# A mixture of experts ahead of three convolution layers: two images per product, gates multiplied into the patches, expert outputs summed feature-major in one PSUM bank

## The reference

```
xp = patches of the normed x                  # 16 * 256 patches, d = 128 features
probs = softmax(xp @ router_w)                # 8 experts
gate = the two largest of probs, divided by their sum, zero elsewhere
for e in range(8):
    val, g = split(xp @ w1[e])                # 2 x 256 hidden features
    out += gate[:, e] * ((val * sigmoid(g)) @ w2[e])
```

## Time and profile before

| | |
|---|---|
| median of 3 runs | 1914.44 us (1912.62 to 1920.05) |
| span of the profiled execution, the time of this execution | 2385.4 us |
| PE busy, products | 1477.8 us (62%) |
| DVE busy | 902.8 us (38%) |
| ACT busy | 513.5 us (22%) |
| POOL busy | 1200.2 us (50%), of it 1147.6 in 1152 gathers |
| mean granted clock of PE | 0.782 of full |

### The profile page before, as it was taken

The page is one execution under the profiler, slowest core; times in us unless marked ns, Lnnn a source line. Parts: engine busy times, 40 slices in busy tenths (PEclk is TensorE's granted clock), DMA queues, the critical chain, the costliest instruction groups (busy, mean ns, idle before and its releaser), DMA issues.

```text
span 2385.4 us, 17778 instructions
## 1 busy us (share of the span) xinstructions
PE 1477.8 (62%) x5782; PEld 846.0 (35%) x5782; DVE 902.8 (38%) x1416; ACT 513.5 (22%) x823; POOL 1200.2 (50%) x1393
## 2 busy tenths in 40 slices
PE   6973323465257966774578985674339684138988
PEld 5842222353133433542244443542114231013433
DVE  3532322234242332575332333576313227441235
ACT  2220000112022223112322322112302221023343
POOL 7126675556744644565654654465664546740000
PEclk9976555677578988886678998786669886568999
DMA  4021111112121111112131111112131111111000
GB/s 169 1 56 43 41 51 39 39 34 80 52 65 35 41 29 35 38 38 76 49 74 32 41 37 33 34 47 66 51 80 32 37 32 43 53 32 44 1 0 9
DMA packets 66784, 106.71 MB, mean 45 GB/s; under 512 B 20480, under 2 KB 43904, under 8 KB 66304
## 3 DMA queue, kind: packets, MB, share of 16 engines
q0 software_dynamic: 36864, 75.57, 11.8%
q1 hardware_dynamic: 29248, 26.81, 4.0%
q10 hardware_dynamic: 576, 3.15, 0.3%
HBM read 83.16 MB, written 13.89 MB: 41 GB/s over the span
## 4 chain that ended last, share of the span: by engine, by line
PE 35%; another core or an unknown queue 28%; issue 14%; DVE 9%; ACT 5%; POOL 3%; DMA 1%; DVEq 0%; SPq 0%; ACTq 0%; POOLq 0%
PE bank L1326 9%; PE bank L1311 8%; PE bank L1226 4%; POOL gt L635 3%; PE bank L1357 3%; PE bank L1236 2%; DVE gt L1038 2%; DVE rb L1117 2%; PE bank L1331 2%; PE bank L1266 2%; PE bank L1344 1%; PE bank L1288 1%; PE bank L1385 1%; DVE gt L1039 1%
## 5 line engine op out<-in xcount | busy, mean ns | idle before, releaser
L635 POOL DMA_INDIRECT gt<-corner_table,idx x1152 | 1147.6, 996 | 920.0 <-DVE sm L1044 490.9
L1226 PE MATMUL bank<-xp,w_sb 128*128 128x256 f32 x1024 | 310.4, 452 | 119.1 <-issue 50.9
L1326 PE MATMUL bank<-yg,wts 128*128 128x512 f32 x512 | 257.3, 647 | 46.9 <-ACT tg L758 38.1
L1226 PEld LDWEIGHTS bank<-xp,w_sb 128*128 128x128 f32 x1024 | 221.5, 229 | 179.1 <-issue 66.2
L1311 PE MATMUL bank<-u,wk 128*128 128x512 f32 x512 | 240.9, 620 | 9.0 <-DMA u<-sqb 9.0
L941 DVE SCALAR_TENSOR_TENSOR he<-he,bank 128x512 f32<-128x512 f32 x128 | 87.7, 685 | 399.2 <-ACT he L692 194.1
L1236 PE MATMUL bank<-w_sb,he 128*128 128x128 f32 x1024 | 159.5, 301 | 115.5 <-issue 101.8
L1357 PE MATMUL bank<-xp,musq 128*128 128x512 f32 x212 | 131.0, 765 | 145.5 <-issue 82.4
L1236 PEld LDWEIGHTS bank<-w_sb,he 128*128 128x128 f32 x1024 | 154.8, 216 | 129.8 <-issue 120.6
L1288 PE MATMUL bank<-cst,sm 128*128 128x128 f32 x384 | 82.5, 330 | 189.2 <-DVE sm L1044 84.5
L1038 DVE TENSOR_TENSOR gt<-gt,cw 128x1152 f32<-128x1152 f32 x128 | 173.2, 1353 | 52.9 <-DMA gt<-corner_table,idx 35.4
(11 more groups left out here) (185 smaller groups left out, 1258.2 us busy)
## 6 DMA issues: line engine op xcount, KB each, us to landing
gt<-corner_table,idx POOLq DMA_INDIRECT x1152
corner_table<-tb SPq DMA_DIRECT2D x45, 256.0 KB, 5.6
u<-sqb SPq DMA_DIRECT2D x64, 128.0 KB
w_sb<-w ACTq DMA_DIRECT2D x2, 1024.0 KB, 9.2
out<-X SPq DMA_DIRECT2D x8, 256.0 KB
X<-x SPq DMA_DIRECT2D x1, 1536.0 KB, 18.8
wts<-weights SPq DMA_DIRECT2D x1, 1446.0 KB, 15.3
w_sb<-w ACTq DMA_DIRECT2D x2, 512.0 KB, 12.1
```

What stands on the lines that cost most here:

```text
L635: pool.indirect_dma_start(gt[:, g, k].rearrange("p a c -> p (a c)"), None, table, bass.IndirectOffsetOnAxis(ap=idx[:, j, g * KK + k:g * KK ...
L1226: op = mm(psum[b][:, h * TOK:(h + 1) * TOK], w1_sb[:, e, first + h], xp[:, g], start=True, stop=True)
L1326: op = mm(psum[B2.bank(name)][:, :], w_glu[:, k, col + d * P:col + (d + 1) * P], yg[:, c % 2, k], start=k == 0, stop=k == NB2 - 1)
```

## The change

A unit is now (pair of images q, expert e, half h of the hidden features), again 32 of them. Gate, value and output are one product of 512 columns each. The gate weights no longer scale the output: before the experts, PE turns the gates so that (patch block, expert) lies on 64 partitions, DVE spreads them to `shares` (64 x 1024) with one block of columns for each block of patches, and for each pair and expert one more product, "share", with a one-hot column as weights, broadcasts a row of gates to 128 partitions of bank 0; DVE multiplies `xp` by it into `xg`, which feeds the value product. The outputs, features on partitions, of all eight experts and both halves add up in bank 2 over 16 units, so `acc` and its additions are gone. ACT copies the bank twice a slice; 16 products with 32 columns of the identity as weights put the features back on the channels' partitions, and DVE adds in two instructions of 512 elements. The order has one part more, `l0_gates`, ahead of the units, and steps 0 to 2 of sampling hold seven parts. Constants grow by 16 columns.

```diff
@@ -19,7 +19,7 @@
-NU = GI * NE
+NU = 2 * NE * 2
@@ -40,7 +40,7 @@
-A_PLACES = [(0, 2, 6), (2, 17, 9), (17, 22.5, NU + 2 - 15), (22.5, 23.6, 2), (25.2, 27.8, 3 + TQ - 2)]
+A_PLACES = [(0, 2, 7), (2, 17, 9), (17, 22.5, NU + 2 - 15), (22.5, 23.6, 2), (25.2, 27.8, 3 + TQ - 2)]
@@ -144,12 +144,12 @@
 def plan_a():
-    plan = [(("xp", 0), 0), (("xp", 1), 1), ("router", 2)]
+    plan = [(("xp", 0), 0), (("xp", 1), 1), ("router", 2), ("turned", 2), (("share", 0), 0)]
     for u in range(NU):
         plan += [(("gate", u), 0), (("value", u), 1)]
-        if u:
-            plan.append((("out", u - 1), 2))
-    plan += [(("out", NU - 1), 2), (("back", 0), 0), (("back", 1), 1)]
+        if u % 2 and u < NU - 1:
+            plan.append((("share", u // 2 + 1), 0))
+    plan += [(("out", q), 2) for q in range(2)] + [(("back", 0), 0), (("back", 1), 1)]
     head = [("omc", 0), ("omc", 1), ("table", 0), ("table", 1), ("om", 0), ("om", 1)]
@@ -181,7 +181,7 @@
-    parts = [("l0_unit", u) for u in range(NU + 1)] + [("l0_tail",), ("l1_norm",), ("l1_conv",), ("l1_om",)]
+    parts = [("l0_gates",)] + [("l0_unit", u) for u in range(NU + 1)] + [("l0_tail",), ("l1_norm",), ("l1_conv",), ("l1_om",)]
@@ -320,9 +320,9 @@
-        acc = sb("acc", [P, 2, PT * PT, GI, C])
-
-        xn0 = acc[:, :, :, :, :].rearrange("p t a g c -> p (t a g c)")
+        xg = sb("xg", [P, 2, HALF])
+
+        xn0 = xg[:, :, :].rearrange("p i n -> p (i n)")
@@ -346,7 +346,10 @@
-        omt = acc[:, :, :, :, :].rearrange("p t a g c -> p (t a g c)")
+        omt = xg[:, :, :].rearrange("p i n -> p (i n)")
+
+        shares = cwn[0:8 * NE, :, :, :].rearrange("p t k a -> p (t k a)")[:, 0:8 * P]
+        oT = [t[:, :, :].rearrange("p t k -> p (t k)")[:, 0:HALF] for t in (fl, fr)]
@@ -686,10 +689,18 @@
                     return
+                if u == NU // 2 + 1:
+                    l0_result(s, 0)
                 B0.filled(act, s, ("gate", u))
-                if u >= 2:
-                    B0.filled(act, s, ("out", u - 2))
+                if u == NU // 2 + 1:
+                    B0.filled(act, s, ("out", 0))
+                elif u >= 2:
+                    act.wait_ge(S["he_used"], s * (NU - 2) + u - 1 - (u - 2) // (NU // 2))
                 act.activation(he[:, u % 2], psum[0][:, :], ACT.Tanh, scale=0.5).then_inc(free[0], 1)
+
+            def l0_result(s, q):
+                B0.filled(act, s, ("out", q))
+                act.activation(oT[q], psum[2][:, :], ACT.Copy).then_inc(free[2], 1)
@@ -932,44 +943,42 @@
-                ch.then(stt(out=gate[:, :, :], in0=gate[:, :, :], scalar=0.5, in1=over(m1),
-                            op0=ALU.mult, op1=ALU.mult))
-
-            def l0_he(s, u):
+                stt(out=gate[:, :, :], in0=gate[:, :, :], scalar=0.5, in1=over(m1),
+                    op0=ALU.mult, op1=ALU.mult).then_inc(S["gate_ready"], 1)
+
+            def l0_gates(s):
+
+                B0.filled(dve, s, "turned")
+                op = tt(shares.rearrange("p (t n) -> p t n", t=8),
+                        psum[2][0:8 * NE, 0:P].unsqueeze(1).to_broadcast([8 * NE, 8, P]),
+                        con("token")[0:8 * NE].unsqueeze(2).to_broadcast([8 * NE, 8, P]), ALU.mult)
+                op.then_inc(free[2], 1)
+                l0_share(s, 0)
+
+            def l0_share(s, i):
+
+                q = i // NE
+                B0.filled(dve, s, ("share", i))
+                tt(xg[:, i % 2], xp[:, 2 * q:2 * q + 2].rearrange("p g n -> p (g n)"), psum[0][:, :], ALU.mult)\
+                    .then_inc(free[0], 1)
+
+            def l0_unit(s, u):
+                if u == NU:
+                    return
                 B0.filled(dve, s, ("value", u))
...
                     op0=ALU.add, op1=ALU.mult).then_inc(free[1], 1)
-
-            def l0_acc(s, u):
-                g, e = divmod(u, NE)
-                B0.filled(dve, s, ("out", u))
-                if e:
-                    B0.read(dve, s, ("out", u - 1))
-                for t in range(2):
-                    sc = gate[:, g * 2 + t, e:e + 1]
-                    o = psum[2][:, t * D0:(t + 1) * D0].rearrange("p (a c) -> p a c", c=C)
-                    a = acc[:, t, :, g]
-                    if e:
-                        op = stt(out=a, in0=o, scalar=sc, in1=a, op0=ALU.mult, op1=ALU.add)
-                    else:
-                        op = ts(a, o, sc, None, ALU.mult)
-                    if t:
-                        op.then_inc(free[2], 1)
+                if u % 2 and u < NU - 1:
+                    l0_share(s, u // 2 + 1)
             def l0_tail(s):
-                for t in range(2):
-                    B0.filled(dve, s, ("back", t))
-                    for dy in range(PT):
-                        xv = X[:, bass.ds(s, 1), :].rearrange("p o (h a w b) -> p (o h) a b w", a=PT, b=PT,
-                                                              w=W // PT)
-                        xv = xv[:, t * 8:(t + 1) * 8, dy].rearrange("p h b w -> p b h w")
-                        bk = psum[t][:, dy * 2 * P:(dy + 1) * 2 * P].rearrange("p (b h w) -> p b h w", b=PT, h=8)
-                        op = tt(xv, xv, bk, ALU.add)
-                        if dy:
-                            op.then_inc(free[t], 1)
-                        else:
-                            ch.did(op)
+                xv = X[:, bass.ds(s, 1), :].rearrange("p o (h a w b) -> p (o h) a b w", a=PT, b=PT, w=W // PT)
+                for dy in range(PT):
+                    B0.filled(dve, s, ("back", dy))
+                    xd = xv[:, :, dy].rearrange("p h b w -> p b h w")
+                    bk = psum[dy][:, :].rearrange("p (b h w) -> p b h w", b=PT, h=H // PT)
+                    tt(xd, xd, bk, ALU.add).then_inc(free[dy], 1)
                 B0.read(dve, s, ("back", 0))
@@ -1218,35 +1221,57 @@
+            def l0_gates(s):
+
+                pe.wait_ge(S["gate_ready"], s + 1)
+                B0.vacant(pe, s, "turned")
+                hold(pe)
+                pe.transpose(psum[2][0:8 * NE, 0:P], gate[:, :, :].rearrange("p t e -> p (t e)"), ident)\
+                  .then_inc(full[2], 1)
+                B0.read(pe, s, "turned")
+                l0_share(s, 0)
+
+            def l0_share(s, i):
+
+                q, e = divmod(i, NE)
+                B0.vacant(pe, s, ("share", i))
+                mm(psum[0][:, :], con("expert")[0:8 * NE, e:e + 1].to_broadcast([8 * NE, P]),
+                   shares[:, q * HALF:(q + 1) * HALF], start=True, stop=True).then_inc(full[0], 1)
+
             def l0_h(s, u):
-                g, e = divmod(u, NE)
-                for kind, b, first in (("gate", 0, 2), ("value", 1, 0)):
-                    B0.vacant(pe, s, (kind, u))
-                    for h in range(2):
-                        op = mm(psum[b][:, h * TOK:(h + 1) * TOK], w1_sb[:, e, first + h], xp[:, g],
-                                start=True, stop=True)
-                    op.then_inc(full[b], 1)
+
+                i, h = divmod(u, 2)
+                q, e = divmod(i, NE)
+                B0.vacant(pe, s, ("gate", u))
+                mm(psum[0][:, :], w1_sb[:, e, 2 + h], xp[:, 2 * q:2 * q + 2].rearrange("p g n -> p (g n)"),
+                   start=True, stop=True).then_inc(full[0], 1)
+                B0.read(pe, s, ("share", i))
+                B0.vacant(pe, s, ("value", u))
+                mm(psum[1][:, :], w1_sb[:, e, h], xg[:, i % 2], start=True, stop=True).then_inc(full[1], 1)
+                if h and u < NU - 1:
+                    l0_share(s, i + 1)
             def l0_out(s, u):
-                g, e = divmod(u, NE)
+                i, h = divmod(u, 2)
+                q, e = divmod(i, NE)
                 B0.read(pe, s, ("value", u))
-                B0.vacant(pe, s, ("out", u))
-                for t in range(2):
-                    for h in range(2):
-                        op = mm(psum[2][:, t * D0:(t + 1) * D0],
-                                he[:, u % 2, h * TOK + t * P:h * TOK + (t + 1) * P], w2_sb[:, e, h],
-                                start=h == 0, stop=h == 1)
-                op.then_inc(full[2], 1)
+                if u % (NU // 2) == 0:
+                    B0.vacant(pe, s, ("out", q))
+                last = u % (NU // 2) == NU // 2 - 1
+                mm(psum[2][:, :], w2_sb[:, e, h], he[:, u % 2], start=u % (NU // 2) == 0, stop=last)\
+                    .then_inc(full[2] if last else S["he_used"], 1)
             def l0_tail(s):
-                B0.read(pe, s, ("out", NU - 1))
-                for t in range(2):
-                    B0.vacant(pe, s, ("back", t))
-                    for dyx in range(4):
-                        op = pe.transpose(psum[t][:, dyx * P:(dyx + 1) * P],
-                                          acc[:, t, dyx].rearrange("p g c -> p (g c)"),
-                                          ident)
-                    op.then_inc(full[t], 1)
+                for q in range(2):
+                    B0.read(pe, s, ("out", q))
```

(30 more changed lines are left out.)

## The result

The kernel after takes 1957.11 us (median of 4 runs, 1955.34 to 1961.69); the kernel before, beside it, 1913.53 us (1911.65 to 1920.05). The ratio is 1.0229, 95% interval 1.0205 to 1.0252: slower by 43.6 us.

A forecast was written before the change was run, and what follows sets the result against it. PE bounds the uncovered head, the gathers' pace nearly bounds the middle. The median 1914.4 plus 20.5 for the head and 18 for two slices gives 1953 us; range 1908 to 1985, the forecast's own 1938 to 1972.

The forecast's parts named there:

- The 471 us: Profiled execution's excess over the runs' median, read mostly as PE holes while gathers run, which ordinary runs lack.
- Head, 20.5 us: First slice's layers 0 and 1 before the first gather: PE-bound, uncovered, 20.5 us longer; bounds 14 to 26.
- The pair: Two units of the first layer in the head: 6.11 us after the change, 3.06 a unit, +0.44 each.
- Middle, 18 us: Two slices with layers 2 and 3 beside them: PE's extra work costs 9 us each, between 0 and 12.3.
- the ring of four: Four places for gathered tiles in the middle: hides PE or DVE lateness up to three steps, 33.7 us.
- the 67 us: Runs' median above head, gathers at 1.248 us and tail; taken as a sign the ring is partly used up.
- DVE's 7.2 us at nothing: DVE works 7.2 us less a slice: worth nothing in the head, in the middle only where DVE ends last.
- B: Only the head counts, the middle stays at the gathers' pace: 1935 us; chance 0.20.
- C: Share product's chain shows in the middle, DVE's multiplication queuing: 48 us over three slices, 1983 us; chance 0.10.
- D: DVE, not PE, ends the dense stretches last; its 7.2 us return in two slices: 1921 us; chance 0.10.
- E: PE holes occur in ordinary runs; fewer instructions return 0.23 of them: 1862 us, in between 1890; chance 0.14.
- F: Wide products are cheap, hand-overs bound the first layer, some 2.1 us a unit: 1906, or 1890 us; chance 0.01.

The follow-up runs named there:

- two kernels with later multiplications: Kernel before with an idle DVE reduction, some 0.5 or about 1.1 us, ahead of each sampling step's multiplication, on another chip: 0.9948 and 1.0217 of the kernel before.
- without the share: Kernel after without share product and multiplication into `xg`, value reading `xp`, gates still spread but unread: 0.9986 of the kernel before.
- the earlier share in bfloat16: Kernel after with the share product issued one unit earlier and gates and one-hot column in bfloat16, on another chip: 0.9982 of the kernel before.
- first experiment: Kernel before, unchanged, timed and profiled once more: 0.9984 of the kernel before, span 1913.8 us.
- the kernel with half of the additions: Kernel before with one of a unit's two `l0_acc` accumulations left out after the first expert: 0.9960 of the kernel before.
- the kernel after with the earlier share: Kernel after with the share product issued one unit earlier, behind the even unit's value product, on another chip: 0.9971 of the kernel before.
- the kernel with the 0.5 us instruction: Kernel before with an idle DVE maximum over 420 columns ahead of each sampling step's multiplication, on another chip: 0.9948 of the kernel before.

## Why the prediction held, and where it didn't

**The 471 us.** Right for the metric: the runs had no such holes. But such holes need not be one execution's own: on the other chip every run is as long, and all four profiles have them. On which chip the profiled execution ran is not on record.

**Head, 20.5 us.** 20.9 measured, by errors that cancel. The pair is 6.40 us, not 6.11: +4.3 over 15 pairs. The gates end at 28.97 us, 2.6 earlier than before, since the logits' 16 instructions start 1.0 earlier and last 1.92 us there instead of 3.55. That is the clock: the kernel after has both in one trace, 1.92 us at a granted clock of 1.00 and, for the same instructions of the next slice, 3.55 at 0.50. Windows of the kernel after, columns as in the earlier trace rows:

```profile
22.00:24.00 2.00, 1.92 (x16) 1.84 (x16) 0.04 (x1) 1.21 (x1) 1.67 (x11) 1.00 1.15 346
183.90:187.40 3.50, 3.50 (x16) 3.45 (x16) 0.00 (x0) 1.20 (x1) 2.59 (x4) 0.50 0.19 50
```

The kernel before has 3.55 us in this place in each of its profiles, but the two kernels with later multiplications have 1.92, and two forms of the change (without the share, and with the earlier share in bfloat16) 3.55. So either level occurs in either kernel, and the gain is luck. (The views print 1.00 there for the kernel before too; its first clock record begins only at 30.9 us.) The first gate product starts at 33.74 instead of 35.2 although PE begins at half clock, which the prediction had not counted (1 us for the share alone). At the end the second copy is followed by 32 instructions that take 1.93 us at a granted clock of 1.00, 0.060 each and not 0.114: the 3.64 us of the earlier trace rows are what such a group takes at 0.50 (at 179.49 us in the kernel after). From unit 31's start at 133.60 to the statistics at 141.07 are 7.5 us: 0.3 less than before, not 1.2 more. And from the statistics to the first gather, where no line is changed, are 39.3 us against 41.6: the offset convolution's 36 instructions take 17.12 us at a granted clock of 0.92 there, 18.45 at 0.85 in the kernel before, first experiment. From start to end: unit 31 starts 23.45 later, then 0.3 and 2.3 come back.

**Middle, 18 us.** 2.8 + 5.9 + 10.4 = 19.1 measured in slices 0 to 2, 16.3 of it in the two slices that the 18 were for. The size fits, within the scatter of one profile, but for a wrong reason. The prediction let the ring of four run out. Ring waits are 8.3 us in one slice only. Against that, gathers are lengthened by 2.7, 5.9 and 3.0 us more in slices 0, 1 and 2. By the counts above these are gathers that DVE lengthens because PE's additional work makes it late. The same holds for the 67 us that the runs had over the gathers' pace: I read them as a ring used up in part, and the first experiment shows none of it.

**DVE's 7.2 us at nothing.** Nearly right: 6.8 us a slice gave 0.4% of the runs, 3 to 12 us, and nothing in the profile.

**The rivals.** B (middle for nothing) fails by 19 us. C (the share's chain) is there but small: 0.10 us a pair, 0.27 in bfloat16. D (DVE ends the dense stretches) wanted 14 us off slices 1 and 2, which grew by 16.3; and the kernel with half of the additions gave back 8 us in all, 12 at most. F is out: a pair takes 6.40, not under 5.24. E is false where the runs were timed and was not foolish: on the chip with holes, the kernel after with the earlier share, which has 18% fewer PE instructions in all (4730 products, not 5782), lost 24 to 27 us in the head (first gather at 183.9 us, against 159.6 and 157.2 in the kernel with the 0.5 us instruction) and had the kernel before's time, 0.9971. The page's first line and its waits there:

```profile
span 2351.4 us, 15507 instructions
...
L638 POOL DMA_INDIRECT gt<-corner_table,idx x1152 | 1169.2, 1015 | 862.7 <-issue 459.5 <-DVE sm L1053 403.2
```

403 us of waits stand against 491, and against 428 in the kernel with the 0.5 us instruction. The price of E, 0.23 of the holes, was still too high: 73 us by the sum, where these runs give 24 to 27 us of head plus 0.0029 x 2342 = 7, some 33, with an interval of 14 us to either side.

## What to carry to other kernels

Weights moved from an output to an input have to be made before the first product, and spread to all partitions: count that product at full width, and the start it delays, against what is saved later. Where gathers issued by GpSimd set the pace, count as well at which phase DVE's instructions with two SBUF inputs meet them: here a late engine cost time with no wait in the profile. A profile that is far longer than the runs may show another chip's habit: profile again before reading its middle, and expect the verdict to hold for the chip it was taken on.

## What the hardware showed that was not expected

- A gather lasts 0.945 us, or until 0.82 us after the end of a two-input SBUF instruction of DVE that it started in, up to 2.16 us; 23 that came within 0.05 us of the start of one, ahead of it at the ports as it seems, kept theirs. All lengthening together is 83.5 us of 1913.8 in the kernel before.
- A fast instruction of DVE with one SBUF input does it too: in the kernel after `xpad` (L990, 128x1024) from 867.74 for 0.82 us, and a gather from 868.04 for 1.33 us.
- Two chips, one program: 1920 and 2342 us, the second with PE standing for no wait that the profile shows. What the cause is stays open.
- The share product (64 rows, one column repeated as weights) starts 0.10 us and the product behind it 0.19 us later than their columns say; the cause stays open.
- The same 16 or 32 instructions take nearly twice as long at a granted clock of 0.50 as at 1.00 (3.55 against 1.92 us, 3.64 against 1.93), and which level the start of the program has differs from one kernel and profile to the next.
